# First stage of an adaLN Mamba-2 block: modulation sections in four 32-column groups, other load order, deeper rings, second batch chain in pieces

## The reference

```python
# B = 4 batches, L = 512 tokens, D = 512; 64 heads of 16, 8 groups, state 64
mod = (silu(c) @ wmod).reshape(4, 6, 1, 512)           # c: 4 x 512, wmod: 512 x 3072
sa, ca, ga, sb, cb, gb = (mod[:, i] for i in range(6))
ga, gb = (sign(g) * max(abs(g), 0.25) for g in (ga, gb))
h = layernorm(x) * (1 + ca) + sa
xBC, z, A_log = split(h @ in_proj_w.T)                 # 2048, 1024 and 64 columns
x, B, C = split(silu(causal_conv4(xBC) + bias))
dt = softplus(A_log)
y = ssd_chunk_scan(x, -dt, B, C) + D * x / dt          # state-space scan
x1 = x0 + ga * ((y * silu(z + z_bias)) @ out_proj_w.T)
out = x1 + gb * ((layernorm(x1) * (1 + cb) + sb) @ binarized(ffn_w).T + b_ffn)
```

## Time and profile before

| | |
|---|---|
| three runs | 722.79 us median (719.93 to 724.25) |
| the profiled execution | 725.2 us, span 723.5 us, mean granted clock 0.963 |
| busy of the span | TensorE 91%, VectorE 71%, ScalarE 52%, GpSimd 52% |
| DMA | 70.53 MB, 97 GB/s on average |

### The profile page before, as it was taken

The page is one execution under the profiler, slowest core; times in us unless marked ns, Lnnn a source line. Parts: engine busy times, 40 slices in busy tenths (PEclk is TensorE's granted clock), DMA queues, the critical chain, the costliest instruction groups (busy, mean ns, idle before and its releaser), DMA issues. The chain is left out here.

```text
span 723.5 us, 21285 instructions
## 1 busy us (share of the span) xinstructions
PE 660.5 (91%) x8347; PEld 497.3 (69%) x8347; DVE 516.7 (71%) x913; ACT 379.1 (52%) x818; POOL 374.9 (52%) x464
## 2 busy tenths in 40 slices
PE   5559797989999999999999999999997999999994
PEld 2244455767777777777777777777775767778783
DVE  3569739796787777777778677777788567676663
ACT  1573633545654545564644564556665545555552
POOL 7544401244653634555445365464556757777771
PEclk9678899999999999999999999999999999999995
DMA  9354211133312121132123143321213755333401
GB/s 265 79 205 121 72 31 54 62 94 106 95 63 93 60 71 65 59 129 67 34 84 104 37 137 107 111 94 49 92 68 101 224 156 153 117 117 117 132 30 43
DMA packets 61915, 70.53 MB, mean 97 GB/s; under 512 B 13972, under 2 KB 33460, under 8 KB 61816
## 3 DMA queue, kind: packets, MB, share of 16 engines
q1 hardware_dynamic: 56376, 69.12, 29.6%
q10 hardware_dynamic: 5440, 0.05, 0.4%
HBM read 54.45 MB, written 14.70 MB: 96 GB/s over the span
## 5 line engine op out<-in xcount | busy, mean ns | idle before, releaser
L1393 DVE SCALAR_TENSOR_TENSOR m_cv<-bank,gpc,m_cv 128x511 f32<-128x511 f32 (+2 forms) x192 | 143.3, 747 | 31.9 <-ACT m_cv L1304 27.3
L1149 PE MATMUL bank<-h_hi,w_hi 128*128 128x512 f32 x384 | 161.0, 419 | 4.8 <-ACT p_hf L647 1.7
L1149 PE MATMUL bank<-h_hi,w_lo 128*128 128x512 f32 x384 | 153.9, 401 | 0.0
L1149 PE MATMUL bank<-h_lo,w_hi 128*128 128x512 f32 x384 | 153.4, 400 | 0.0
L1528 POOL TENSOR_TENSOR m_S<-m_S,m_cd 128x128 f32<-128x128 f32 x96 | 39.7, 413 | 159.3 <-DVE m_S L1453 80.2
L1304 ACT ACTIVATE m_cv<-bank,gpc 128x512 f32<-128x512 f32 x96 | 71.8, 748 | 76.5 <-PE bank L1149 76.5
L1149 PEld LDWEIGHTS bank<-h_hi,w_hi 128*128 128x128 f32 x384 | 74.4, 194 | 20.7 <-issue 6.8
L1149 PEld LDWEIGHTS bank<-h_hi,w_lo 128*128 128x128 f32 x384 | 73.8, 192 | 17.3
L1518 POOL TENSOR_TENSOR m_Xw<-m_Xp,wend 128x256 f32<-128x256 f32 x64 | 39.8, 621 | 87.8 <-ACT m_Xp L1324 87.8
L1149 PEld LDWEIGHTS bank<-h_lo,w_hi 128*128 128x128 f32 x384 | 74.4, 194 | 14.1
L1316 ACT ACTIVATE m_M<-bank 128x512 f32<-128x512 f32 x128 | 76.2, 595 | 12.4 <-PE bank L1158 10.4
(11 more groups left out here) (172 smaller groups left out, 1283.8 us busy)
## 6 DMA issues: line engine op xcount, KB each, us to landing
m_ea<-ea_scratch SPq DMA_DIRECT2D x32, 256.0 KB
m_dd<-dd_scratch SPq DMA_DIRECT2D x32, 256.0 KB
y_scratch<-m_t SPq DMA_DIRECT2D x16, 512.0 KB, 3.3
h_lo_place<-y_scratch SPq DMA_DIRECT2D x16, 512.0 KB, 4.3
p_wm<-in_L_wmod_dram SPq DMA_DIRECT2D x6, 1024.0 KB, 8.1
m_wraw<-in_L_attn_in_proj_w_dram SPq DMA_DIRECT2D x18, 256.0 KB, 3.1
p_xt<-in_L_attn_input__dram SPq DMA_DIRECT2D x16, 256.0 KB, 5.2
w_lo_place<-in_L_attn_input__dram SPq DMA_DIRECT2D x16, 256.0 KB, 4.5
```

Source lines behind the costliest of these rows:

```text
L1149: ins = pe.matmul(A[k % 3][:, :], w[:, t, kc, :], h[:, n % NB, kc, :], start=(m == 0), stop=(m == 11))
L1393: ins = dve.scalar_tensor_tensor(out=cv[:, k % 3, lag:], in0=A[k % 3][:, 0:L - lag], scalar=s.gpc[:, gp, o:o + 1], in1=cv[:, k % 3, lag:], ...
```

## The change

- Sections: the four matmuls of a section go to four groups of 32 columns (partitions 32k to 32k+31), each with its own sum; `scT` is padded with zeros to 32 columns. `turn_section` becomes four fp32 matmuls with a 0/1 matrix `pick` of 128x4, which adds the four groups.
- Loads: sections 0 and 1 first, then the `A_log` rows and tiles 0 to 7; `x` has a ring of 8 (the second four in memory of the second chain), normalized tiles a ring of 4, statistics have 16 places. Sections 4 and 5 are loaded into the places of `x` (`last_sections`).
- Order: `wa_lo` ahead of all normalizing; tiles 12 to 15 normalized by GpSimd; statistics of 12 to 15 ahead of `softplus(0)`; `skips(0)` to the end of the stage; other PSUM banks, so that `project(0)` and `project(1)` no longer wait for the third batch; sections 2 and 3 behind the last weights; `dt_inputs(1)` ahead of the last two `turn_section`.
- The chain of batches 2 and 3: `softplus(1)` in slot 3 of unit -1, `finish_times(1)` in unit 0, `sums(1)` in unit 1 (was -1), `low_sums(1)` in unit 2 (was 1), `skips(1)` in unit 4 (was 3).

```diff
     def row_bank(n):
-        return s.bank[(4, 5, 0, 1, 1, 3)[n]]
+        return s.bank[(7, 6, 1, 3, 1, 3)[n]]
...
             for k in range(KC):
-                ins = pe.matmul(row_bank(n)[0:NB, :], scT[:, k, :], wm[:, n % 2, k, :], start=(k == 0), stop=(k == KC - 1))
+                ins = pe.matmul(row_bank(n)[32 * k:32 * k + 32, :], scT[:, k, :], wm_of(n)[:, k, :], start=True, stop=True)
...
             pe.wait_ge(sec_cp, n + 1)
+            pe.wait_ge(picked, KC + 1)
             for k in range(KC):
-                ins = pe.transpose(mod_bank(n)[:, k * NB:(k + 1) * NB], row_of(n)[:, k * P:(k + 1) * P], s.ident[0:NB, 0:NB])
+                ins = pe.matmul(mod_bank(n)[:, k * NB:(k + 1) * NB], row_of(n)[:, k * P:(k + 1) * P], pick[:, :], start=True, stop=True)
...
+    def last_sections(sp):
+
+        sp.wait_ge(ln_n, 16)
+        for n in (4, 5):
+            sp.dma_start(wm_of(n), w_mod.rearrange("(k p) n -> p k n", p=P)[:, :, SEC[n] * D:(SEC[n] + 1) * D]).then_inc(d_wm[n % 2], 16)
...
         constant_fills()
-        for i in range(4):
+        constant_shapes()
+        for i in range(5):
             root(i)
-        constant_shapes()
-        root(4)
+        low_part(0)
         root(5)
-        low_part(0)
+        low_part(2)
         root(6)
-        low_part(2)
         root(7)
...
+        for i in range(8, 16):
+            root(i)
+        weights(4)
+        weights(5)
+        for i in range(12, 16):
+            normalize(i)
+        weights(6)
+        weights(7)
+        pool.wait_ge(a_v[0], A_END)
         low_part(8)
         low_part(10)
...
                     if (v, sl) == (-1, 3):
+                        start.softplus(dve, 1)
+                    if (v, sl) == (0, 3):
+                        start.finish_times(dve, 1)
+                    if (v, sl) == (1, 3):
                         start.sums(dve, 1)
-                    if (v, sl) == (1, 3):
+                    if (v, sl) == (2, 3):
                         start.low_sums(dve, 1)
-                    if (v, sl) == (3, 3):
+                    if (v, sl) == (4, 3):
                         start.skips(dve, 1)
```

More of the change, by code:

```diff
@@ L538, in vector @@
         low_part(13)
+        convolve(2)
         low_part(15)
-        convolve(2)
         silu(1)
@@ L547, in vector @@
         gates()
-        softplus(dve, 1)
-        finish_times(dve, 1)
+        skips(dve, 0)
     def chained(dve, pb, count):
@@ L687, in scalar @@
         softplus_inputs(0)
+        make_h(8)
+        make_h(9)
+        weights(4)
+        weights(5)
+        make_h(10)
+        make_h(11)
+        linear(0)
+        weights(6)
+        weights(7)
+        linear(1)
+        decays(act, 0)
+        linear(2)
+        tanh(0)
+        make_h(12)
+        make_h(13)
+        tanh(1)
+        make_h(14)
+        make_h(15)
         for n in range(8, 12):
-            make_h(n)
-        for n in range(4, 8):
             weights(n)
-        linear(0)
-        decays(act, 0)
         copy_row(2)
         copy_row(3)
-        linear(1)
-        for n in range(12, 16):
-            make_h(n)
-        linear(2)
-        tanh(0)
-        for n in range(8, 12):
-            weights(n)
-        tanh(1)
         linear(3)
@@ L794, in weights @@
             ins.then_inc(wt_pe, 1)
-        pe.wait_ge(sct_ready, 1)
+        pe.wait_ge(cond_step, 4)
+        section(0)
+        section(1)
         pe.wait_ge(d_wa, 16)
         for k in range(KC):
-            ins = pe.transpose(DTB[:, k * NH:(k + 1) * NH], wa_raw[:, k * P:(k + 1) * P], s.ident[0:NH, 0:NH])
+            ins = pe.transpose(s.bank[5][:, k * NH:(k + 1) * NH], wa_raw[:, k * P:(k + 1) * P], s.ident[0:NH, 0:NH])
         ins.then_inc(wa_pe, 1)
-        turn(0)
-        turn(1)
-        section(0)
-        turn(2)
-        turn(3)
-        section(1)
+        pe.wait_ge(sec_cp, 2)
         turn_section(0)
         turn_section(1)
-        for i in range(4, 8):
+        for i in range(8):
             turn(i)
@@ L812, in tensor @@
             weights(n)
-        pe.wait_ge(wa_dve, 1)
         dt_inputs(0)
-        pe.wait_ge(w_act, 4)
         for i in range(8, 12):
             turn(i)
-        for n in range(4, 8):
-            weights(n)
+        weights(4)
+        weights(5)
         project(0, 0)
         project(0, 1)
+        project(1, 0)
+        project(1, 1)
+        weights(6)
+        weights(7)
+        project(2, 0)
+        project(2, 1)
+        for i in range(12, 16):
+            turn(i)
+        for n in range(8, 12):
+            weights(n)
         section(2)
         section(3)
-        project(1, 0)
-        project(1, 1)
+        project(3, 0)
+        project(3, 1)
         turn_section(2)
         turn_section(3)
-        for i in range(12, 16):
-            turn(i)
-        project(2, 0)
-        project(2, 1)
-        for n in range(8, 12):
-            weights(n)
-        project(3, 0)
-        project(3, 1)
         section(4)
         section(5)
-        pe.wait_ge(w_act, 12)
         end_turn(pe, 0)
+        pe.wait_ge(h_act, 16)
+        dt_inputs(1)
         turn_section(4)
         turn_section(5)
-        dt_inputs(1)
         pe.wait_ge(gate_v, 3)
@@ L1062, in sync @@
             start.sync(sp)
+            start.last_sections(sp)
             sp.wait_ge(start.kcopy, 4)
```

224 lines of the change are left out of this document (112 added, 112 removed).

## The result

The changed kernel takes 726.87 us in the median of 13 runs (724.59 to 728.4), the kernel before 724.22 in 13 runs on the same chip: ratio 1.0045, 95% interval 1.0023 to 1.0066. It is slower by some 3.3 us, where 4.9 less were forecast. A later set of runs of the same two kernels gave 1.0053 (1.0034 to 1.0073), 3.8 us.

What follows compares the result with a forecast made beforehand. It took waits to bound the first stage and TensorE the main loop. The entry 4.2 us earlier plus 0.7 in the loop gave 4.9 us off the median 722.8: 718 us, own range 715 to 721, wider range 712.5 to 724.5.

Steps and rivals of the forecast that it cites:

- A_END to entry: From the end of VectorE's first softplus chain to the loop's first projection: 33.7 us, 6.5 shorter than 40.25.
- the start: Loads to first decay products, `dt_inputs(0)`: 2.3 us later than before, putting the first softplus chain's end near 65.3.
- the loop: Second batch pair's chain in pieces: unit 6 62.0 us behind the loop's first projection, before 62.7; 0.7 us gained.
- The first copy: ScalarE's first copy in the start, behind its load issues: at 19.8, bounds 18.9 to 20.6.
- The join: `turn_section` of sections 0 and 1 in the start, adding the column groups: 1.2 us a pair, bounds 0.8 to 3.
- The first decay products: `dt_inputs(0)` on TensorE, end of the start: from 41.9, where they began at 39.59 before.
- the ring: x tiles 0 to 7 loading from the first microsecond, slowing ScalarE's issues: first copy at 19.8 for 18.9.
- GpSimd's normalizing: Tiles 12 to 15 on GpSimd: 1.0 us per `tensor_scalar`, bounds 0.66 to 1.67; 0 to 1.5 on the chain, taken 0.
- cover of 10 us: GpSimd's normalizing ends at about 62, 10 us before `make_h(12)` may run near 72, so it costs nothing.
- The column groups: Four 32-column matmuls run side by side: a section takes 0.9 us at full clock, 1.75 at half.
- the start eats it: Rival 1: ScalarE's issues end at 22 or the turns queue at half clock; end 721 to 723.5; chance 0.18.
- an A_END after 67: Sign of being wrong: the first softplus chain on VectorE ends after 67, where the forecast had near 65.3.

Runs made afterwards that it cites:

- before_again: The kernel before, unaltered, profiled once more and timed against itself; ratio 1.0018 (0.9995 to 1.0042).
- a_hfirst: Changed kernel with `make_h(12..15)` placed ahead of the first two tanh on ScalarE; ratio 1.0008 against the kernel before.
- a_start: Changed kernel with the start in the order of before (x tiles loaded first, tiles 0 to 3 turned around the two sections); ratio 1.0053 against the kernel before.
- a_hring: Changed kernel with `make_h(12..15)` ahead of two tanh, the start's old order, and x tiles 4 to 7 loaded one by one; ratio 0.9935 against the kernel before.
- a_vnorm: Changed kernel with statistics and normalizing of tiles 12 to 15 back on VectorE behind the first pair's sums; ratio 1.0098 against the kernel before.
- b_pieces: Kernel before with only the second pair's softplus and what follows it in five pieces inside units 0 to 4; ratio 0.9985.
- a_warm: Changed kernel with 28 unread matrix products put into TensorE's idle time from 69.5 to 84.5; ratio 1.0067 against the kernel before.
- a_join: Changed kernel with six unread 512-column products on TensorE ahead of the join of sections 0 and 1; ratio 1.0033 against the kernel before.

## Why the prediction was wrong

Set against before_again, the sum of the prediction misses 8.0 and 8.5 us at unit 8 (it had -4.9, the two profiles have +3.1 and +3.6). The chain of waits was largely the one that I had described; what failed are the sizes of its terms: A_END to entry by 5.6 and 4.9 us, the start by 2.5 and 2.4, the loop up to unit 8 by -0.1 and 1.2.

- **"A_END to entry: 6.5 us shorter than 40.25."** Two errors of about one size. The 40.25 came from one execution with its clock at 0.83, and I took the difference off the median, 722.8, as if the usual run had such a stretch: 2.5 us (40.25 less 37.72). I had noted that this execution was 2.4 above the median, and did not ask where it was so. The rest is the walk: 33.7 forecast, 36.84 and 36.09 measured. In the first profile `tanh(0)` ended at +7.7, not +6.0, since two low parts ahead of it took 2.88 us on VectorE (one alone takes 0.69, at 78.49) while GpSimd, late by its normalizing, did its own two in 3.38 (the last two rows of the second list of the result). `project(3)` took 0.4 more than forecast, and the two pairs of `turn_section` 1.84 us each at a granted clock of 1.00, where I had 1.2. That `make_h(12)` stands behind `tanh(0)`, with an idle TensorE, I had seen and costed at 6 us; a_hfirst shows that 2.3 to 3.1 of them come back at the entry by a change of order.
- **"The start: 2.3 us later."** It is 4.8 at A_END (68.07 and 67.96 against 63.24). The first copy was right (19.8 forecast, 19.50). The join was mis-sized, 1.2 us for 3.58, outside my bounds, which took both prices at one clock. The first decay products came at 43.68, not 41.9, which is 4.9 behind before_again's 38.78, and the chain began only at 54.67 behind the four statistics, though its input was there at 53.5. The experiments divide this: with the order of before they start at 41.35 (a_start), and with the deep ring unused as well at 37.53 (a_hring). In these single profiles the ring, which I had at the 0.9 us by which the first copy comes later, is the larger part. How it acts behind the copy is not shown.
- **"GpSimd's normalizing: 1.0 us."** It is 2.46, outside my bounds, 0.66 to 1.67. Of the cover of 10 us 6.8 were used up: the last tile is at 68.83 where I had 62. Its effect on the chain beside it, 0 to 1.5 us by my bounds, I took at 0, and the four statistics ahead of the chain too: a_vnorm, with both moved behind the chain, has its A_END 2.8 us earlier. The same run shows that the place on GpSimd gains even so.
- **"The loop: 0.7 gained."** Right where it is alone: 61.90 us to unit 6 in b_pieces, 61.98 in the first profile, 62.0 forecast. In the second profile of the changed kernel it is 63.26, with a granted clock of 0.68 from 105 to 110.

The column groups were right: by rows I had 0.9 us for a section at full clock and 1.75 at half, and 1.04 to 1.06 and 1.82 were measured. The Trainium skill, page TensorE: Matmul & The Clock Gate, section "Measured speedup vs the span model", by which I had 1.1, is nearer; the trace agrees with it. Of the rivals the first, the start eats it, comes nearest, but its condition did not come about (the issues ended at 19.5, not 22), and with 721 to 723.5 it was too small as well. Of the signs of being wrong, one came true: an A_END after 67.

## What to carry to other kernels

Before a forecast rests on one profile, compare its own time with the median and find the stretch that is off (a granted clock of 0.83 where 1.00 is usual was 2.5 us here, about half of the forecast gain). A deeper ring can make a start later: leaving it unused there brought the decay products 3.35 us forward and the time down by some 3 us, although the bytes were the same. Look at what else runs while the loads flow. And when an instruction waits for another engine, ask what stands behind it on its own: eight copies moved ahead of two tanh were worth some 3 us, about as much as all the work on the sections (3.4).

## What the hardware did that I had not expected

- The recorded clock doesn't always tell TensorE's speed, and the duration of a known instruction helps. In the changed kernel it is 1.00 from 4 to 28 us, but a section takes 1.94 us there (at 6.5) and the join 3.58, where at 93.35, also at 1.00, a section takes 1.06 and at 91.58 the join 1.84. In a_hring a section takes 1.94 at 11.91 and, behind it, 1.07 at 15.21, all at a recorded 1.00.
- GpSimd's `tensor_scalar` with two operands by partition, 128x512, takes 2.46 us beside a busy VectorE (2.65 in the second profile), whose chained operations take 0.89 us each in the same time (4.47 for five; 0.79 in the earlier trace rows).
- Filling TensorE's idle time raised the clock behind it once (a_warm, 0.83 for 0.62 and 0.52) and not the other time (a_join, 0.50 from 22 to 26 us behind 6.7 us of products).
